# Slots of sorted edges: a sum over 25 node blocks by a tree of additions instead of a reduce, and integer shifts instead of rounding

## The reference, cut to what matters

```python
edge_in = jnp.concatenate([h[row], h[col], dist], axis=1)
e = jax.nn.silu(edge_in @ eW1 + eb1)
e = jax.nn.silu(e @ eW2 + eb2)
agg = jax.ops.segment_sum(e, row, num_segments=h.shape[0])
node_in = jnp.concatenate([h, agg], axis=1)
out = jax.nn.silu(node_in @ nW1 + nb1) @ nW2 + nb2
x = _layernorm(x + out, axis=-1)
```

## Time and profile before

| What | us |
|---|---|
| median of 3 runs | 631.85 |
| span of the profiled execution | 629.0 |
| PE busy | 530.9 (84%) |
| DVE busy | 463.5 (74%) |
| POOL busy | 429.0 (68%) |
| ScalarE (ACT) busy | 355.5 (57%) |
| gathers on POOL (line 736), 440 | 419.4 |

### The profile page before, as it was taken

The page is one execution under the profiler, slowest core; times in us unless marked ns, Lnnn a source line. Parts: engine busy times, 40 slices in busy tenths (PEclk is TensorE's granted clock), DMA queues, the critical chain, the costliest instruction groups (busy, mean ns, idle before and its releaser), DMA issues.

```text
span 629.0 us, 15166 instructions
## 1 busy us (share of the span) xinstructions
PE 530.9 (84%) x4653; PEld 447.6 (71%) x4653; DVE 463.5 (74%) x1364; ACT 355.5 (57%) x812; POOL 429.0 (68%) x465
## 2 busy tenths in 40 slices
PE   4942869879879989998998899889997888879795
PEld 3421658768768869887887778778776777769684
DVE  6987999988999899989888869797642533223356
ACT  5842555455555556755655555565556666656464
POOL 2337576566777777777777777777777777777750
PEclk9986899779999999999999999999999999999997
DMA  5211111111111121111121111111111121111111
GB/s 121 77 51 51 43 52 48 36 50 48 56 52 52 52 56 56 52 56 49 54 56 52 51 55 56 53 52 55 54 54 55 52 56 54 53 55 53 55 39 51
DMA packets 17215, 34.17 MB, mean 54 GB/s; under 512 B 8133, under 2 KB 9352, under 8 KB 17142
## 3 DMA queue, kind: packets, MB, share of 16 engines
q0 software_dynamic: 14080, 28.86, 16.0%
q1 hardware_dynamic: 2594, 3.40, 2.1%
q10 hardware_dynamic: 468, 0.96, 0.6%
HBM read 30.73 MB, written 2.40 MB: 53 GB/s over the span
## 4 chain that ended last, share of the span: by engine, by line
POOL 32%; DVE 25%; PE 21%; issue 16%; DMA 3%; DVEq 1%; SPq 0%; POOLq 0%
POOL q_rows L736 32%; PE layer_ps L749 9%; PE sort_ps L749 6%; PE seg_ps L749 5%; DVE load_hot L1212 3%; DVE agg L1283 3%; DVE count L1058 2%; DMA q_rows<-q_table,q_index 2%; DVE hot L1268 2%; DVE col_hot L1206 1%; DVE row_hot L1207 1%; DVE place L1102 1%; PE turn_ps L841 1%; DMA src_i<-in_src_dram 1%; DVE slot L1108 1%
## 5 line engine op out<-in xcount | busy, mean ns | idle before, releaser
L736 POOL DMA_INDIRECT q_rows<-q_table,q_index x440 | 419.4, 953 | 159.5 <-issue 127.6
L583 ACT ACTIVATE e<-layer_ps 128x512 f32<-128x512 f32 x110 | 65.7, 597 | 212.7 <-PE seg_ps L749 204.3
L1283 DVE TENSOR_TENSOR agg<-agg,seg_ps 128x125 f32 x416 | 93.3, 281 | 93.5 <-PE seg_ps L749 90.3
L749 PE MATMUL layer_ps<-hotT,p_table 128*128 128x128 bf16 x1320 | 158.8, 225 | 0.2
L749 PE MATMUL layer_ps<-ident_f,q_rows 128*128 128x128 f32 x440 | 126.7, 288 | 33.6 <-DMA q_rows<-q_table,q_index 32.8
L749 PE MATMUL seg_ps<-hot,e 128*128 128x125 f32 x880 | 125.1, 286 | 23.9 <-DVE agg L1283 23.9
L749 PEld LDWEIGHTS layer_ps<-hotT,p_table 128*128 x1320 | 122.3, 98 | 22.7 <-issue 2.3
L749 PEld LDWEIGHTS seg_ps<-hot,e 128*128 128x128 f32 x880 | 109.5, 196 | 27.3 <-issue 25.3
L749 PE MATMUL layer_ps<-w_sb,h 128*128 128x128 f32 x880 | 119.5, 279 | 0.0
L749 PEld LDWEIGHTS layer_ps<-w_sb,h 128*128 128x128 f32 x880 | 111.2, 193 | 4.6 <-issue 0.2
L749 PEld LDWEIGHTS layer_ps<-ident_f,q_rows 128*128 128x128 f32 x440 | 63.0, 143 | 44.3 <-DMA q_rows<-q_table,q_index 43.3
(11 more groups left out here) (193 smaller groups left out, 439.9 us busy)
## 6 DMA issues: line engine op xcount, KB each, us to landing
q_rows<-q_table,q_index POOLq DMA_INDIRECT x440
q_table<-q_in_sb SPq DMA_DIRECT2D x1, 784.0 KB
x_sb<-in_x_dram ACTq DMA_DIRECT2D x1, 700.0 KB
q_table<-q_in_sb SPq DMA_DIRECT2D x1, 616.0 KB
out_dram<-x_sb SPq DMA_DIRECT2D x2, 224.0 KB
out_dram<-x_sb SPq DMA_DIRECT2D x1, 252.0 KB
w_in<-in_edge_weight_dram SPq DMA_DIRECT2D x1, 185.9 KB
dst_i<-in_dst_dram SPq DMA_DIRECT2D x1, 185.9 KB
```

The lines of the kernel that those rows point to most:

```text
L583: A.activation(e2[:, m % 2, :], e_of(m)[:], ACT.Silu).then_inc(e2_ready, 1)
L736: P.indirect_dma_start(q_rows[:, g % RING, j, :], None, q_table, bass.IndirectOffsetOnAxis(ap=q_index[:, GT * g + j:GT * g + j + 1], axis= ...
L749: return nc.tensor.matmul(o, lhsT, rhs, start=start, stop=stop, **kw)
L1283: D.tensor_tensor(o, o, seg_ps[:, j * LO:(j + 1) * LO], ALU.add).then_inc(agg_added, 1)
```

## The change

SCAN runs on over all 25 blocks: the second instruction starts with the last count of the first. `count` has one more element, a zero ahead, so that the count ahead of a block is the element before it, also for the first; TOTAL therefore reads both ends straight from `count`, and `run_end` and `run_prev` go. The one in PSUM is written once, ahead of the wait for the sources, into `const_ps`. SUM has one tile `place` for all columns: part 0 is one addition and one multiplication over everything, part 1 sums the 25 blocks by additions in place (12 to 12, 6 to 6, 3 to 3, then blocks 2 and 24 onto 0 and 1, and last 1 onto 0, written as int32). `base` has 63 * 128 added, so that places stay positive; SLOTS takes tile and slot apart with int32 shifts and a mask, in eight instructions instead of ten. `nodes` reads the int32 sources directly, without a cast to f32 first.

```diff
--- before.py
+++ after.py
@@ -61,9 +61,10 @@
 
 LAYERS = 3
 ENC = 8192
+TOP = ENC // SLOT - 1
 TAG = 1 << 29
 assert sum(LOAD) == ECOL and TILES % GT == 0 and all(n % 2 == 0 for n in LOAD[:-1]) and V * CMAX <= 512
-assert all(EP * COL0[k] // SLOT + FULL[k] <= TABLE for k in range(CHUNKS)) and EP * max(LOAD) + SLOT <= 8000
+assert all(EP * COL0[k] // SLOT + FULL[k] <= TABLE for k in range(CHUNKS)) and EP * max(LOAD) + SLOT <= TOP * SLOT
 
 
 def chunk_of(g):
@@ -279,15 +280,16 @@
         load = sb("load", [EP, ECOL, V, 2], BF16)
 
         in_win = sb("in_win", [EP, WIN * NMAX], BF16)
-        count = sb("count", [EP, WIN * NMAX], BF16)
-        place = [sb(f"place{i}", [EP, WIN * (NMAX // 2)]) for i in range(2)]
-        slot, tile, up, whole, delta = (sb(n, [EP, NMAX]) for n in ("slot", "tile", "up", "whole", "delta"))
+        count = sb("count", [EP, 1 + WIN * NMAX], BF16)
+        place = sb("place", [EP, WIN * NMAX])
+        slot_i, tile_i, whole_i, upto_i = (sb(n, [EP, NMAX], I32) for n in ("slot_i", "tile_i", "whole_i", "upto_i"))
+        col_f, other_f, moved_f = (sb(n, [EP, NMAX]) for n in ("col_f", "other_f", "moved_f"))
         col2 = sb("col2", [EP, NMAX, 2], BF16)
         row2 = sb("row2", [EP, NMAX, 2], BF16)
 
-        total, run_end, run_prev, rank, carried, summed, rounded, tiles, tiles_upto, base = (
+        total, rank, carried, summed, rounded, tiles, tiles_upto, base = (
             sb(name, [EP, WIN]) for name in (
-                "total", "run_end", "run_prev", "rank", "carried", "summed", "rounded", "tiles", "tiles_upto", "base"))
+                "total", "rank", "carried", "summed", "rounded", "tiles", "tiles_upto", "base"))
         dest_row = sb("dest_row", [1, V, WIN])
         dest_t = sb("dest_t", [1, 2, WIN])
         dest_col = sb("dest_col", [V * WIN, 1])
@@ -347,7 +349,6 @@
         def bank_of(k):
             return k % 2 if k else 1
 
-        one_ps = [t[0:EP, 511:512] for t in flat_ps]
         layer_ps = [ps(f"layer_ps{i}", [128, 512]) for i in range(LAYERS)]
         seg_ps = ps("seg_ps", [128, 512])
         const_ps = ps("const_ps", [128, 512])
@@ -365,6 +366,7 @@
         iota1_c = const_ps[:, 64:128].bitcast(BF16)
         iota_w_c = const_ps[0:EP, 128:128 + WIN].bitcast(BF16).rearrange("p (b e) -> p b e", e=2)
         base_c = const_ps[0:EP, 160:160 + WIN]
+        one_c = const_ps[0:EP, 511:512]
         nb2_c = const_ps[0:LO, 408:408 + NF]
         mean_c = const_ps[0:LO, 472:472 + WIN]
 
@@ -690,7 +692,7 @@
             P.iota(part_i[:], pattern=[[0, 1]], base=0, channel_multiplier=1).then_inc(iotas_ready, 1)
             P.iota(iota_i[:], pattern=[[1, 512]], base=0, channel_multiplier=0).then_inc(iotas_ready, 1)
             P.iota(dest_i[:], pattern=[[128, V], [1, WIN]], base=0, channel_multiplier=0).then_inc(iotas_ready, 1)
-            fills = [(ones[:], 1.0), (run_prev[:], 0.0), (carried[:], 0.0), (win_b[:, ECOL:ECOL + 1], -1.0),
+            fills = [(ones[:], 1.0), (count[:, 0:1], 0.0), (carried[:], 0.0), (win_b[:, ECOL:ECOL + 1], -1.0),
                      (queue_f[:], 0.0), (eps_sb[:], EPS)]
             zeros = [(w1_sb[NF:2 * NF, :, 0, :], 0.0), (w1_sb[0:NF, :, 1, :], 0.0), (xT[NF:2 * NF, len(PAIRS) - 1, :], 0.0),
                      (n1x_sb[NF:2 * NF, 0, :], 0.0), (n1x_sb[0:NF, 1, :], 0.0)]
@@ -1015,10 +1017,9 @@
 
             def nodes(a, b):
 
-                then(D.tensor_copy(node_f[:, a:b], src_i[:, a:b]))
-                then(D.tensor_scalar(lo_t[:, a:b], node_f[:, a:b], 1.0 / WIN, -(WIN // 2) / WIN, ALU.mult, ALU.add))
+                then(D.tensor_scalar(lo_t[:, a:b], src_i[:, a:b], 1.0 / WIN, -(WIN // 2) / WIN, ALU.mult, ALU.add))
                 then(D.tensor_scalar(lo_f[:, a:b], lo_t[:, a:b], ROUND, -ROUND, ALU.add, ALU.add))
-                then(D.scalar_tensor_tensor(win_b[:, a:b], lo_f[:, a:b], -float(WIN), node_f[:, a:b], ALU.mult, ALU.add))
+                then(D.scalar_tensor_tensor(win_b[:, a:b], lo_f[:, a:b], -float(WIN), src_i[:, a:b], ALU.mult, ALU.add))
 
             def encode(a, b):
 
@@ -1038,7 +1039,8 @@
                     residual(i)
                     return
                 n, m, c0 = LOAD[k], EVEN[k], COL0[k]
-                win3, count3 = (t[:, 0:WIN * m].rearrange("p (b t) -> p b t", b=WIN) for t in (in_win, count))
+                win3, before3, count3 = (t.rearrange("p (b t) -> p b t", b=WIN) for t in (
+                    in_win[:, 0:WIN * m], count[:, 0:WIN * m], count[:, 1:1 + WIN * m]))
                 full = float(FULL[k])
                 if name == MATCH:
                     shape = [EP, WIN, m // 2, 2]
@@ -1049,27 +1051,21 @@
                 elif name == SCAN:
                     a, b = (m * w for w in WSPLIT[i])
 
-                    one = one_ps[k % 2]
-                    if i == 0:
-                        if k >= 2:
-                            dve.wait_ge(w_parted, k - 1)
-                        then(D.tensor_copy(one, ones[0:EP, 0:1]))
-                    done(scanned[k, 0])
+                    if i == 0 and k >= 2:
+                        dve.wait_ge(w_parted, k - 1)
+                    done(scanned[k, i])
                     scanned[k, i + 1] = mark(D.tensor_tensor_scan(
-                        count[:, a:b], one.to_broadcast([EP, b - a]), in_win[:, a:b], 0.0, ALU.mult, ALU.add))
+                        count[:, 1 + a:1 + b], one_c.to_broadcast([EP, b - a]), in_win[:, a:b], count[:, a:a + 1],
+                        ALU.mult, ALU.add))
                 elif name == TOTAL:
                     done(scanned[k, 2])
-                    mark(D.tensor_copy(run_end[:], count3[:, :, m - 1]))
-                    for a, b in WSPLIT:
-                        last = mark(D.tensor_copy(run_prev[:, a + 1:b], count3[:, a:b - 1, m - 1]))
-                    done(last)
-                    D.tensor_tensor(total[:], run_end[:], run_prev[:], ALU.subtract).then_inc(totals_ready, 1)
-                    then(D.tensor_tensor(rank[:], carried[:], run_prev[:], ALU.subtract))
+                    D.tensor_tensor(total[:], count3[:, :, m - 1], before3[:, :, 0], ALU.subtract).then_inc(totals_ready, 1)
+                    then(D.tensor_tensor(rank[:], carried[:], before3[:, :, 0], ALU.subtract))
                 elif name == OFFSET:
 
                     dve.wait_ge(offsets_ready, k + 1)
                     then(D.tensor_tensor(summed[:], carried[:], all_ps[k % 2], ALU.add))
-                    mark(D.scalar_tensor_tensor(base[:], earlier_ps[k % 2], -1.0, rank[:], ALU.add, ALU.add))
+                    mark(D.scalar_tensor_tensor(base[:], earlier_ps[k % 2], TOP * SLOT - 1.0, rank[:], ALU.add, ALU.add))
                     then(D.tensor_scalar(rounded[:], summed[:], 1.0 / SLOT, -(SLOT / 2 - 0.5) / SLOT, ALU.mult, ALU.add))
                     then(D.tensor_scalar(tiles[:], rounded[:], ROUND, -ROUND, ALU.add, ALU.add))
                     mark(D.tensor_tensor_scan(tiles_upto[:], ones[0:EP, 0:WIN], tiles[:], 0.0, ALU.mult, ALU.add))
@@ -1095,33 +1091,32 @@
                     D.tensor_copy(queue_i[:, 1:2], queue_f[:, 1:2]).then_inc(dest_ready, 1)
                     dve.wait_ge(dest_ready, 1)
                 elif name == SUM:
-                    halves = [(0, m // 2), (m // 2, m)]
-                    p3 = [place[h][:, 0:WIN * (b - a)].rearrange("p (b t) -> p b t", b=WIN) for h, (a, b) in enumerate(halves)]
+                    p3 = place[:, 0:WIN * m].rearrange("p (b t) -> p b t", b=WIN)
                     if i == 0:
-                        for h, (a, b) in enumerate(halves):
-                            added[h] = mark(D.tensor_tensor(
-                                p3[h], count3[:, :, a:b], (base_c if k else base[:]).unsqueeze(2).to_broadcast([EP, WIN, b - a]), ALU.add))
-                    a, b = halves[i]
-                    done(added[i])
-                    mark(D.tensor_tensor(p3[i][:, 0:HALF], p3[i][:, 0:HALF], win3[:, 0:HALF, a:b], ALU.mult))
-                    then(D.tensor_tensor(p3[i][:, HALF:WIN], p3[i][:, HALF:WIN], win3[:, HALF:WIN, a:b], ALU.mult))
-                    picked[i] = mark(D.tensor_reduce(slot[:, a:b], p3[i].rearrange("p b t -> p t b"), AX.X, ALU.add))
+                        then(D.tensor_tensor(p3, count3, (base_c if k else base[:]).unsqueeze(2).to_broadcast([EP, WIN, m]), ALU.add))
+                        added[k] = mark(D.tensor_tensor(p3, p3, win3, ALU.mult))
+                        return
+
+                    done(added[k])
+                    for into, of in ((slice(0, 12), slice(12, 24)), (slice(0, 6), slice(6, 12)), (slice(0, 3), slice(3, 6)),
+                                     (slice(0, 2), slice(2, 25, 22))):
+                        then(D.tensor_tensor(p3[:, into], p3[:, into], p3[:, of], ALU.add))
+                    picked[k] = mark(D.tensor_tensor(slot_i[:, 0:m], p3[:, 0], p3[:, 1], ALU.add))
                 elif name == SLOTS:
-                    done(picked[1])
```

(30 more changed lines are left out.)

## The result

The changed kernel takes 625.85 us, median of four runs (624.99 to 627.83); the kernel before, run beside it, 631.88 (631.36 to 632.32). The ratio is 0.9921, with a 95% interval of 0.9900 to 0.9942. So it is faster, by 6.0 us by the medians and by 5.0 by the ratio, where 2.6 were forecast: in the range, but under the likeliest case's own range (627.8 to 630.6). On another chip the ratio was 0.9928 (0.9913 to 0.9943), which is 4.6 us.

What follows compares the result with a forecast made beforehand. The prediction took POOL's stream of 440 gathers, one every 1.25 us, plus its waits, to bound the kernel. Its terms -1.1 - 4.2 + 2.7 = -2.6 took 631.85 to 629.2 us, range 624.5 to 634.0.

Steps and rivals of the forecast that it cites:

- the likeliest case: The forecast without its rivals, given 40%: 629.2 us, with a range of its own of 627.8 to 630.6.
- The front: Time until POOL's first gather: 1.1 us less, the gather at 38.2 instead of 39.27; bounds 0.5 and 1.9.
- the ring argument: Chunk 0: the sixth one-hot batch waits for PE's third sort (ring of three); first gather at 37.4 or 38.7 refutes it.
- POOL's waits: POOL waiting for PE's matmuls: DVE savings in chunks 1 to 3 take off 4.2 us by 145 us; bounds 2 and 14.
- The holds: Gathers stalled by DVE instructions with two SBUF inputs: 0.67 us more in each of chunks 5 to 8, 2.7 in all.
- The sum: Whole span: -1.1 - 4.2 + 2.7 = -2.6 us, from 631.85 to 629.2.
- (b): PE keeps its upper clock after idle; POOL can use 2 us of that in its waits: 627.2 us; 20%.
- (c): Holding gathers costs nothing more because phases fall well: -5.3 us, 626.5; 12%.
- (a): SUM's tree of additions holds a gather as one: hold cost 8.8 us, +3.5 in all, 635.3, slower; 15%.
- (d): First gather 0.5 us earlier, and PE, not DVE, sets half of POOL's waits: 631.9 us, no change; 13%.
- The scans: DVE's scans, now with a start value from SBUF: gathers getting slower there would make the prediction wrong.

Runs made afterwards that it cites:

- kernel 7: The change in chunks 4 to 8 only, the other chunks as in the kernel before: 630.47 us, ratio 0.9998.
- kernel 12: The kernel before with 44 added PE matmuls that nothing reads, in chunk 3's idle stretch (step 13) alone: 630.38 us, ratio 0.9980.
- kernel 3: The changed kernel with one more unused product of two SBUF operands ahead of the addition in chunks 4 to 8: 629.26 us, ratio 0.9968.
- Kernel 5: The change in chunk 0 only, chunks 1 to 8 as in the kernel before: 629.89 us, ratio 0.9985.
- kernel 6: The change in chunks 0 to 3 only, chunks 4 to 8 as in the kernel before: 625.85 us, ratio 0.9926.
- kernel 1: The changed kernel run again without an edit: 626.79 us, ratio 0.9928.
- kernel 2: The changed kernel with the multiplication of place by in_win cut into five pieces in chunks 4 to 8: 624.2 us, ratio 0.9888.
- kernel 4: The changed kernel with one more unused sum, one operand in PSUM, ahead of the addition in chunks 4 to 8: 625.73 us, ratio 0.9908.
- kernel 10: The changed kernel with the multiplication in five pieces, and a reduce and a copy for the tree, in chunks 4 to 8: 623.72 us, ratio 0.9878.
- kernel 11: The change in chunks 0 to 3 only, with added PE matmuls that nothing reads: 624.02 us, ratio 0.9888.
- kernel 8: The changed kernel with 44 PE matmuls that nothing reads in each of two idle stretches of PE: 623.8 us, ratio 0.9898.

## Why the prediction was right about the sign, and what was off in the sum

**The front: 1.1 forecast, 0.8 from the change.** The first gather came 1.73 earlier, but not by the change alone: x landed 0.97 earlier in this execution, and that varies from run to run (6.49 to 7.66 in the profiles). PE's first matmuls on it, before and then after:

```profile
7.46 2.76 PE L793 MATMUL layer_ps<-ident_f,x_sb 125*128 125x125 f32 x12 [7.46 <-DMA x_sb<-in_x_dram]
```

```profile
6.49 2.76 PE L795 MATMUL layer_ps<-ident_f,x_sb 125*128 125x125 f32 x12 [6.49 <-DMA x_sb<-in_x_dram]
```

So the 37.54, near the 37.4 that was to refute the ring argument, says little by itself; with x as late as before it would be 38.5, between the 38.2 of the forecast and the 38.7 that was to refute it from the other side. From that matmul to the first gather the old front took 31.81, 31.90 and 32.06 us (before, kernels 7 and 12), the new one 30.92 to 31.33, mean 31.15, in ten profiles (all but kernel 3): 0.8 us. Kernel 5 gives 0.15% (interval from 0.3% faster to nothing). The wait of 0.44 for PE's sort shows that the ring set the end. What DVE saves ahead of it was over-counted: the two scans that now follow each other take 3.08 us together instead of 2.81, where I had put 0.1, and the cast saved with them is small.

**POOL's waits: 4.2 forecast, 4.0 measured.** The last real wait of the early stretch ends at 144.07 instead of 149.78, 5.71 earlier; 1.73 of it is the front. What is left, 3.98, is what the change in chunks 1 to 3 gave, with the holds of these chunks (2.64 us instead of 0.52 before 130 us) swallowed by the waits, as the prediction had it. Kernels 5 and 6 put it in the same place: 0.6% between them. From the first gather to the last real wait, the kernels with the old chunks 1 to 3 (before, 5 and 7) took 109.4 to 110.5 us, those with the new ones and no added matmuls (after, 1 to 4, 6 and 10) 105.7 to 106.6, on average 3.7 less. How the gain is split between TOTAL, SUM and SLOTS no run tells. (SUM before had eight instructions, not the ten that the prediction counts; its 5.91 us are read as a whole, so nothing hangs on it.)

**The holds: +2.7 forecast, +0.1 measured.** This is the step that failed, and by its size, not its mechanism. From the last real wait on, the rest of the stream took 458.5 us before and 458.6 after; kernels 7 and 11 say the same in time. Single executions lie up to 1 us around that (457.7 to 459.6), but the averages agree: 458.7 in the five profiles with the old chunks 4 to 8 (before, 5, 6, 11 and 12), 458.6 in the four with the new ones as they are (after, 1, 7 and 8). The holds are there. DVE and POOL of the kernel after, in two chunks:

```profile
211.12 1.57 DVE L1097 TENSOR_TENSOR place<-place,in_win 125x1350 f32<-125x1350 f32 x1
...
214.50 0.81 DVE L1103 TENSOR_TENSOR place<-place 125x648 f32<-125x648 f32 x1
...
268.37 1.56 DVE L1097 TENSOR_TENSOR place<-place,in_win 125x1350 f32<-125x1350 f32 x1
...
271.75 0.81 DVE L1103 TENSOR_TENSOR place<-place 125x648 f32<-125x648 f32 x1
```

```profile
211.85 1.65 POOL L738 DMA_INDIRECT q_rows<-q_table,q_index  x1 [0.30 <-issue]
...
215.05 1.09 POOL L738 DMA_INDIRECT q_rows<-q_table,q_index  x1 [0.30 <-issue]
...
268.94 1.82 POOL L738 DMA_INDIRECT q_rows<-q_table,q_index  x1 [0.30 <-issue]
...
272.31 1.08 POOL L738 DMA_INDIRECT q_rows<-q_table,q_index  x1 [0.30 <-issue]
```

The gathers of 211.85 and 268.94 stood still to the very end of the multiplication (212.69 and 269.93) and lost 0.71 and 0.88; those of 215.05 and 272.31 lost 0.15 and 0.14 over the first addition of the tree. In chunks 5 to 8 the multiplications cost 3.2 us, 0.8 a chunk as estimated, and the tree 0.56, 0.14 a chunk where I had 0.27: 3.8 with a small one. The 0.14 is not an average over chance places: a held gather goes on at the end of the multiplication, the second one behind it starts 2.36 to 2.38 us after that end in all four chunks, and so meets the first addition at the same point. In kernel 2, where no whole multiplication lines the gathers up, the same addition cost 0.2, 0.55 and 0.55, and 0.97 where `dest_hot` ran into it. Before, the same chunks lost 2.3 (1.11 of it by the gather at 282.21), not the 1.6 that I took. That leaves +1.5. Against it stand three small things that I had not in the sum: chunk 4 loses 0.4 instead of 0.55, the small waits near 190 us (0.72) are gone, and holds by the node network behind 560 us fell from 0.83 to 0.28, which is where gathers happen to stand. 1.5 - 0.15 - 0.72 - 0.55 = 0.1. Over the same nine profiles the holds behind the last real wait (by over 0.03 us) are 4.1 us with the new chunks and 3.1 with the old, and the small waits near 190 us 0 and 0.9. So the change made the holds 1.0 us longer, not 2.7: too little was taken for the old ones and too much for the tree. Of the 1.0, 0.9 came back from small waits that the sum had set against chunk 4 alone.

**The sum.** Forecast -1.1 - 4.2 + 2.7 = -2.6. Measured -0.8 - 4.0 + 0.1 - 0.15 and -1.0 for x's earlier landing (rounded), -5.8. The 1.0 is chance; without it the terms make 4.85, near the 5.0 and 4.6 of the two ratios. Kernel 1's profile, where x landed 0.81 earlier, is 4.0 under before's; its normal gathers, 0.003 us longer, cost it 1 us. The time lies under the likeliest case's own range, and in the full one only because that takes in (b) and (c), neither of which is what happened.

**The rivals.** (a), the tree as one hold, is refuted: in the kernel after, behind 150 us no gather lost more than 0.15 in a tree, and the largest loss ahead of that, 0.44 at 81.67 us, was over with the first addition; so were the 0.55 and 0.97 of kernel 2. (c), holds that cost nothing more, came nearest by its time (626.5), but not because holding cost nothing more: the holds grew, and the small waits near 190 us shrank. (b), PE's clock, is half true. In the profile after, the matmuls that took 2.03 behind 3.18 us have 1.13 behind an idle time of 1.07. But kernel 1 has them at 1.64, and those at 116.12 at 1.88, and its waits (9.15) and the end of its last (144.5) are the same: the gain doesn't rest on the clock that came back. What was still to be had from it kernel 8 shows in its traces; what it is worth in the kernel before stays open (kernel 12). (d), PE sets half of POOL's waits, is refuted by the 4.0.

**The scans.** I had named them as what would make the prediction wrong, since they now take a start value from SBUF. 17 gathers met one in the trace after and none was longer than normal.

**Which operands hold a gather.** Two SBUF operands do, one in PSUM doesn't: 2.98 us of standing gathers under the products of kernel 3, none under the sums of kernel 4. The Trainium skill (SBUF — State Buffer, "Who interferes with whom") infers that a tensor_tensor with both inputs in SBUF doesn't stall the generation of descriptors; these runs contradict it. The same section says of DVE's two-port modes that whoever issues first has the port for the whole instruction; the tree agrees with one instruction at a time, since the gathers that met it went on at the end of its first addition.

## What to carry to other kernels

Find the engine whose instructions space out evenly (here POOL, one gather in 1.25 us), and price an edit by the waits of that engine that it shortens: the same edit was worth 4 us in chunks 1 to 3, 0.8 in the front and nothing in chunks 4 to 8, though behind 300 us alone it saved DVE 5 us of work. Where DVE has time to spare, as here behind 150 us, a long instruction with two SBUF operands beside indirect gathers is better cut into pieces with a wait between than made whole (kernel 2, 2.6 us), and an operand in PSUM spares the gathers (kernel 4 against kernel 3). Two edits that each shorten the same stream of gathers need not give the sum: measure them together.

## What was not expected of the hardware

A scan whose start value is an element of SBUF was dearer than one that starts with a constant: 702 elements a partition took 1675 ns instead of 1620, 648 took 1560 instead of 1499. The result's place, one element on, is not the cause: in the late chunks of kernel 6, written to the same place with a constant start, the two took 1622 and 1502. The factor's tile in PSUM changed, too, and no run parts that from the start value. By shape, after and then before:

```profile
L1057 DVE TENSOR_TENSOR_SCAN count<-const_ps,count,in_win 125x702 bf16<-125x702 f32 x4 | 6.7, 1675 | 0.0
...
L1057 DVE TENSOR_TENSOR_SCAN count<-const_ps,count,in_win 125x648 bf16<-125x648 f32 x4 | 6.2, 1560 | 0.0
```

```profile
L1058 DVE TENSOR_TENSOR_SCAN count<-sort_ps,in_win 125x702 bf16<-125x702 f32 x4 | 6.5, 1620 | 0.1
...
L1058 DVE TENSOR_TENSOR_SCAN count<-sort_ps,in_win 125x648 bf16<-125x648 f32 x4 | 6.0, 1499 | 0.0
```

A gather that is held continues with the end of the one instruction that holds it, and 1.56 us of DVE cost it up to 1.21 (kernel 4, the gather at 336.28); where two such instructions overlap, as at 215.46 in kernel 2, it stood to the end of the second. And the instructions with int32 in and f32 out that had no row before cost as much as those in f32: 0.21 us for 50 elements a partition.
